# A fused image/text block on one core: mixer centring folded into the projection weights, attention normalisation taken from the inverse deviation before it

## The reference

```python
h = concat(patch_projection(x) + pos_emb, txt)        # 1 + 196 + 77 tokens
# mixer: two selective scans (forward, backward) over the tokens
xn = layernorm(h)                                     # no gain, no offset
r  = xn + mamba_fwd(xn) + mamba_bwd(xn)               # each ends in a projection (out_proj)
h2 = h + (r - mean(r)) * rsqrt(var(r) + eps) * ln_g + ln_b
# transformer block on a normalised input
x  = layernorm(h2)
x  = x + attention(ln(x) * n1_g + n1_b)               # 12 heads of 16 channels
x  = x + mlp(ln(x) * n2_g + n2_b)                     # erf-gelu, 768 hidden
out = h2 + x
```

## Time and profile before

| | |
|---|---|
| median of 3 runs | 6137.19 us (6126.9 to 6150.05) |
| span of the profiled execution | 6123.8 us (13.4 below the median) |
| DVE busy | 5554.8 us, 91% |
| PE busy | 5309.5 us, 87%, granted clock 0.874 of full |
| ACT busy | 3780.6 us, 62% |
| DMA | 16.6% of 16 engines on the main queue |

### The profile page before, as it was taken

One profiled execution on the slowest core, in us unless ns is written; L12 is line 12 of the kernel. 1 busy time (PEld: TensorE's weight loads), 2 busy tenths in 40 slices (PEclk: granted clock), 3 DMA queues, 4 the chain that ended last, 5 costly groups with the idle time before them and its releaser, 6 DMA issues.

```text
span 6123.8 us, 74116 instructions
## 1 busy us (share of the span) xinstructions
PE 5309.5 (87%) x22816; PEld 3509.9 (57%) x22816; DVE 5554.8 (91%) x6069; ACT 3780.6 (62%) x9506; POOL 0.8 (0%) x8
## 2 busy tenths in 40 slices
PE   5788888888888888888889999888998989989888
PEld 3555555555555555555556655655656556556554
DVE  6999999999999999999999999998999989999962
ACT  3566666656666556666666666666666666666643
POOL 0000000000000000000000000000000000000000
PEclk7898888888888888888989988898888888889885
DMA  3211211211211211211221111111111212112100
GB/s 101 64 45 57 64 45 53 66 51 51 64 52 46 66 58 44 65 53 44 65 65 42 60 60 38 64 58 44 64 45 54 66 37 65 50 47 65 40 23 2
DMA packets 56934, 327.85 MB, mean 54 GB/s; under 512 B 13246, under 2 KB 15742, under 8 KB 23627
## 3 DMA queue, kind: packets, MB, share of 16 engines
q1 hardware_dynamic: 56490, 322.53, 16.6%
HBM read 313.52 MB, written 8.98 MB: 53 GB/s over the span
## 4 chain that ended last, share of the span: by engine, by line
PE 40%; DVE 33%; issue 20%; ACT 6%; DVEq 1%; DMA 0%; SPq 0%; ACTq 0%
DVE hs L953 12%; PE y_ps L417 10%; PE f_ps L530 7%; DVE hs L936 4%; PE f_ps L542 4%; DVE hs L957 4%; PE f_ps L581 3%; PE f_ps L496 2%; PE a_ps L455 2%; DVE neg_max L1062 2%; DVE xc L1016 2%; PE f_ps L511 2%; PE f_ps L592 2%; PE f_ps L487 2%; PE a_ps L465 1%
## 5 line engine op out<-in xcount | busy, mean ns | idle before, releaser
L953 DVE TENSOR_TENSOR_SCAN hs<-decay,hs 128x2192 f32<-128x2192 f32 x384 | 1811.1, 4717 | 28.0 <-issue 19.7
L417 PE MATMUL y_ps<-hs,ident 128*128 128x274 f32 x5376 | 1719.8, 455 | 89.5 <-issue 31.3
L715 ACT ACTIVATE decay<-dt,inner_s 128x273 f32<-128x273 f32 x3072 | 1380.6, 513 | 75.7 <-issue 40.3
L417 PEld LDWEIGHTS y_ps<-hs,ident 128*128 128x128 f32 x5376 | 1104.1, 217 | 480.8 <-issue 187.8
L936 DVE TENSOR_TENSOR hs<-b_rows,dtu 128x2192 f32<-128x2192 f32 x384 | 935.5, 2436 | 99.2 <-PE y_ps L417 76.7
L957 DVE TENSOR_TENSOR hs<-hs,c_rows 128x2192 f32<-128x2192 f32 x384 | 934.7, 2434 | 3.4
L530 PE MATMUL f_ps<-qk 16*92 16x274 f32 x2304 | 733.5, 458 | 227.9 <-ACT hid L788 216.4
L805 ACT ACTIVATE hid<-f_ps 92x273 f32<-92x273 f32 (+1 forms) x1152 | 421.7, 393 | 556.6 <-PE f_ps L542 552.4
L788 ACT ACTIVATE hid<-f_ps,neg_max 92x274 f32<-92x274 f32 x1152 | 544.0, 480 | 301.1 <-DVE neg_max L1062 300.9
L530 PEld LDWEIGHTS f_ps<-qk 16*92 16x92 f32 x2304 | 350.7, 174 | 549.2 <-ACT hid L788 344.6
L542 PE MATMUL f_ps<-ident,hid 92*92 92x92 f32 x3456 | 514.7, 286 | 86.8 <-ACT hid L805 48.7
(11 more groups left out here) (103 smaller groups left out, 5773.8 us busy)
## 6 DMA issues: line engine op xcount, KB each, us to landing
b_rows<-bc_rows SPq DMA_DIRECT2D x128, 1096.0 KB, 5.6
c_rows<-bc_rows SPq DMA_DIRECT2D x128, 1096.0 KB, 5.6
xp<-in_patches SPq DMA_DIRECT2D x32, 588.0 KB, 7.4
out<-h SPq DMA_DIRECT2D x32, 205.5 KB, 2.2
bc_rows<-bc_s SPq DMA_DIRECT2D x64, 34.2 KB, 1.5
h<-in_txt SPq DMA_DIRECT2D x32, 57.8 KB, 2.3
w_in_s<-in_w_in SPq DMA_DIRECT2D x1, 1152.0 KB
fc_s<-in_fc SPq DMA_DIRECT2D x2, 576.0 KB
```

The source lines that it names most:

```text
L417: mm = pe.matmul(y_ps[:, 0:T], ident[:, :], hs[q % 2][:, n, :], start=(q % 2 == 0 and n == 0), stop=(q % 2 == 1 and n == end - 1))
L715: e = act.activation(decay[half][:, n, t], dt[d][:, u, t], ACT.Exp, scale=inner_s[:, d, u, s:s + 1])
L953: dve.tensor_tensor_scan(i, a, i, 0.0, ALU.mult, ALU.add).then_inc(scan_done, 1)
```

## The change

1. Once, at the start, DVE subtracts from every row of `w_out` its mean over the 192 output channels (6 sums, 1 scaling, 6 subtractions). The mixer's output, and with it `res`, then has mean zero. LayerNorm 0 no longer needs its centring matmuls: ACT squares `res` straight from SBUF at gap 4, and DVE scales `res` from SBUF.
2. LayerNorm 2 loses its centring matmuls, its squares and its mean-of-squares matmuls. In their place ACT computes `rstd_n` from `rstd_f` with three activations (`second_rstd`), and DVE scales `res` from SBUF.
3. The gap constants move: LayerNorm 0 ends at gap 5 (6 before), LayerNorm 1 at 7 (8), LayerNorm 2 at 8 (10), and everything from QK on is two gaps earlier, so that the fine part ends at gap 38 instead of 40. In the step of b+1 the last two pieces (`add_mlp`, `last_sum`) so stand at gaps 1 and 2 instead of 3 and 4.

```diff
-        CONSTS = 20
+        CONSTS = 29
-        CENTRE_GAPS = (5, 7, 9, 32)
-        VAR_GAPS = (6, 8, 10, 33)
-        QK_GAPS = (11, 17, 22)
+        CENTRE_GAPS = (6, 30)
+        VAR_GAPS = (5, 7, 31)
+        N1_GAP = 8
+        QK_GAPS = (9, 15, 20)
...
-        PROJ_GAP = 30
-        FC1_GAPS = (34, 35)
-        GELU_GAP = 36
-        FC2_GAPS = (37, 38)
+        PROJ_GAP = 28
+        FC1_GAPS = (32, 33)
+        GELU_GAP = 34
+        FC2_GAPS = (35, 36)
+        ADD_GAP = 37
...
+            def second_rstd(f):
+                wait(act, f_y, at(f, 4, -1))
+                act.wait_ge(f_rstd, at(f, 3, 2))
+                act.activation(rstd_n[:, :], rstd_f[:, :], ACT.Square, scale=EPS ** 0.5).then_inc(n1_step, 1)
+                act.wait_ge(n1_step, at(f, 2, 1))
+                act.activation(rstd_n[:, :], rstd_n[:, :], ACT.Ln, scale=-1.0, bias=n1_c[:, 0:1]).then_inc(n1_step, 1)
+                act.wait_ge(n1_step, at(f, 2, 2))
+                act.activation(rstd_n[:, :], rstd_n[:, :], ACT.Exp, scale=-0.5).then_inc(n1_rstd, 1)
...
+                if gap == 4:
+                    squares(res[:, :, :], sq_f, r_ready, at(f, 1, 1), f_sq)
...
-                    scale_by((cen, res, cen, cen)[j], f_ps[0:CH, 0:2, 0:T], rstd_f, f_rstd, at(f, 4, j + 1), f_y)
+                    scale_by((cen, res, cen)[j], (res[:, :, :], f_ps[0:CH, 0:2, 0:T], f_ps[0:CH, 0:2, 0:T])[j],
+                             rstd_f, f_rstd, at(f, 3, j + 1), f_y)
...
+                if gap == N1_GAP:
+                    dve.wait_ge(f_y, at(f, 4, 2))
+                    scale_by(cen, res[:, :, :], rstd_n, n1_rstd, at(f, 1, 1), f_y)
+                    affine(f, 0, small)
...
+                for u in range(UNITS):
+                    dve.tensor_reduce(out_mean[:, u:u + 1], w_out_s[:, u // IC, u % IC, :], AX_X, ALU.add)\
+                        .then_inc(s_c, 1)
...
+                for u in range(UNITS):
+                    a = dve.tensor_scalar(w_out_s[:, u // IC, u % IC, :], w_out_s[:, u // IC, u % IC, :],
+                                          out_mean[:, u:u + 1], None, ALU.subtract)
```

More of the change, by code:

```diff
@@ L155, in build @@
         rstd_f = sb("rstd_f", [CH, T])
+        rstd_n = sb("rstd_n", [CH, T])
+        out_mean = sb("out_mean", [128, UNITS])
+        n1_c = sb("n1_c", [CH, 1])
         xi = sb("xi", [128, IC, XI_W])
@@ L239, in build @@
         f_rstd = sem("f_rstd")
+        n1_step = sem("n1_step")
+        n1_rstd = sem("n1_rstd")
         f_y = sem("f_y")
@@ L280, in build @@
         SP_PARTS = ((0, 2), (2, 3))
-        CENTRE_GAPS = (5, 7, 9, 32)
-        VAR_GAPS = (6, 8, 10, 33)
-        QK_GAPS = (11, 17, 22)
-        V_GAP = 12
-        SCORE_GAPS = [13 + hd + hd // 4 for hd in range(HEADS)]
-        TURN_GAPS = [gap + 2 for gap in SCORE_GAPS]
-        AV_GAPS = (19, 24, 29)
-        PROJ_GAP = 30
-        FC1_GAPS = (34, 35)
-        GELU_GAP = 36
-        FC2_GAPS = (37, 38)
+        CENTRE_GAPS = (6, 30)
+        VAR_GAPS = (5, 7, 31)
+        N1_GAP = 8
+        QK_GAPS = (9, 15, 20)
+        V_GAP = 10
+        SCORE_GAPS = [11 + hd + hd // 4 for hd in range(HEADS)]
+        TURN_GAPS = [gap + 2 for gap in SCORE_GAPS]
+        AV_GAPS = (17, 22, 27)
+        PROJ_GAP = 28
[3 more added lines that the diff above has]
+        ADD_GAP = 37
         VARIANTS = [(CH, 2, (0, 1)), (CH, 1, (2,)), (C // 3, 1, (0,))]
@@ L500, in f_var_mm @@
             def f_var_mm(f, j):
-                pe.wait_ge(f_sq, at(f, 4, j + 1))
+                pe.wait_ge(f_sq, at(f, 3, j + 1))
                 mean_mm(f_ps[:, 2, :], sq_f, f_var)
@@ L597, in fine_early @@
             def fine_early(f, small, gap):
-                if gap == 40 and small:
+                if gap == ADD_GAP + 1 and small:
                     fc2_mms(f, small, 2, (0,))
@@ L604, in fine_early @@
                     j = CENTRE_GAPS.index(gap)
-                    f_centre_mm(*[(res, r_ready, at(f, 1, 1)), (h2, h2_ready, at(f, 1, 1)), (res, f_y, at(f, 4, 2)),
-                                      (res, x3_step, uneven(f, small, 2, 5, 5 if small else 2))][j])
+                    f_centre_mm(*[(h2, h2_ready, at(f, 1, 1)),
+                                  (res, x3_step, uneven(f, small, 2, 5, 5 if small else 2))][j])
                 if gap in VAR_GAPS:
@@ L832, in fine_mid @@
                     j = VAR_GAPS.index(gap)
-                    rstd(f_ps[0:CH, 2, 0:T], rstd_f, f_var, at(f, 4, j + 1), f_ln, at(f, 4, j + 1), f_rstd)
+                    rstd(f_ps[0:CH, 2, 0:T], rstd_f, f_var, at(f, 3, j + 1), f_ln, at(f, 3, j + 1), f_rstd)
+                    if j == 1:
+                        second_rstd(f)
                 if gap == QK_GAPS[0]:
@@ L844, in fine_late @@
                     j = CENTRE_GAPS.index(gap)
-                    squares(f_ps[0:CH, 0:2, 0:T], sq_f, f_cen, at(f, 4, j + 1), f_sq)
+                    squares(f_ps[0:CH, 0:2, 0:T], sq_f, f_cen, at(f, 2, j + 1), f_sq)
+                if gap == 4:
+                    squares(res[:, :, :], sq_f, r_ready, at(f, 1, 1), f_sq)
                 if gap in QK_GAPS[1:]:
@@ L1133, in fine @@
                     j = VAR_GAPS.index(gap)
-                    scale_by((cen, res, cen, cen)[j], f_ps[0:CH, 0:2, 0:T], rstd_f, f_rstd, at(f, 4, j + 1), f_y)
+                    scale_by((cen, res, cen)[j], (res[:, :, :], f_ps[0:CH, 0:2, 0:T], f_ps[0:CH, 0:2, 0:T])[j],
+                             rstd_f, f_rstd, at(f, 3, j + 1), f_y)
                     if j == 0:
                         add_mixer(f)
-                    if j >= 2:
-                        affine(f, j - 2, small)
+                    if j == 2:
+                        affine(f, 1, small)
+                if gap == N1_GAP:
+                    dve.wait_ge(f_y, at(f, 4, 2))
+                    scale_by(cen, res[:, :, :], rstd_n, n1_rstd, at(f, 1, 1), f_y)
+                    affine(f, 0, small)
                 if gap in SCORE_GAPS:
@@ L1144, in fine @@
                     add_attention(f, small)
-                if gap == 39:
+                if gap == ADD_GAP:
                     add_mlp(f, small)
-                if gap == 40:
+                if gap == ADD_GAP + 1:
                     last_sum(f, small)
@@ L1208, in front @@
                                           ALU.mult).then_inc(s_c, 1)
+                for u in range(UNITS):
+                    dve.tensor_reduce(out_mean[:, u:u + 1], w_out_s[:, u // IC, u % IC, :], AX_X, ALU.add)\
+                        .then_inc(s_c, 1)
+                dve.wait_ge(s_c, 26)
+                dve.tensor_scalar(out_mean[:, :], out_mean[:, :], 1.0 / C, None, ALU.mult).then_inc(s_c, 1)
+                dve.memset(n1_c[:, :], 1.0 + EPS).then_inc(s_c, 1)
+                dve.wait_ge(s_c, 28)
+                for u in range(UNITS):
+                    a = dve.tensor_scalar(w_out_s[:, u // IC, u % IC, :], w_out_s[:, u // IC, u % IC, :],
+                                          out_mean[:, u:u + 1], None, ALU.subtract)
+                a.then_inc(s_c, 1)
                 dve.wait_ge(s_c, CONSTS)
```

## The result

The changed kernel is slower: 6214.94 us median (6206.68 to 6222.78) against 6132.05 for the kernel before on the same chip, ratio 1.0127 with a 95% interval of 1.0093 to 1.0161 (the plain quotient of the two medians is 1.0135, inside that interval). The span of the profiled execution is 6204.9 us, 81.1 more than the 6123.8 of before. Lines have moved: 496 is now 503 (centring), 405 is 412 (mean of squares), 487 is 494 (out-projection), 581 is 588 (fc1), 936 is 956, 953 is 973, 957 is 977, 983 is 1003, 715 is 722.

What follows compares the result with a forecast made beforehand. DVE, busy 91%, and its waits were taken as the bound. Large elements -34, small without MLP -29, MLP +91, drain -10, start +4 gave +22 us: span 6146, about 6159 us median, range 6080 to 6215.

Steps and rivals of the forecast that it cites:

- Scalings from SBUF: Two of DVE's four scalings read SBUF instead of PSUM: 718 ns against 716 ns, no gain.
- LayerNorm 3 at gap 31: DVE's wait at the scaling goes, as the mean of squares precedes the out-projection: gain 1.75 us per element.
- State sums at gap 30: DVE's wait for PE's state sums shrinks at gap 30: gain 1.3 us per element, bounds 0.5 and 1.9.
- LayerNorm 0: Gaps 4 to 6: DVE waits 1.3 us; large elements gain 0.3 us, small ones lose 1.3.
- Heads: First heads at gaps 11, 12: 0.5 us waits; last heads leaving gaps 25 to 27: 0.7 back per small element.
- MLP of a small element: Next step's gaps 0 and 1: DVE waits 3.2 us for state sums, 3.7 for exponentials; loss 6.3 without a jump.
- rival C: TensorE's clock falls at fc1 and gap 32's out-projection: some 2 us for each of 30 elements, 6218 us; chance 0.15.
- MLP of a large element: Same count with 12 rows per fc1 group: loss 0.2 us, or 1.2 at TensorE's low clock; 0.7 taken.
- Behind the jump: Where the loop jumps (5 of 14 places), 14 us of DVE waits against 7.0 before: loss 7.0 each.
- Drain and start: Drain gains 10 us from shorter exposed LayerNorm chains; constants at the start lose 4 us ahead of PE's first matmul.
- Rival B: The MLP block finds room and costs nothing at gaps 0 and 1: -69 us, 6068 us; chance 0.20.
- Rival D: Nothing on the path: gains and losses go into other waits of DVE, 6137 us; chance 0.05.

Runs made afterwards that it cites:

- e8: e3 with 16 matmul rows that nobody reads added at gap 4, ahead of LayerNorm 0's mean of squares; 6075.43 us, ratio 0.9911 to the kernel before.
- e2: The changed kernel with only fc1, GELU, fc2 and the last adds put back to gaps 34 to 40; 6119.76 us, ratio 0.9974 to the kernel before.
- e3: The changed kernel with the out-projection of the first four units at gap 31 instead of 32, ahead of fc1; 6106.06 us, ratio 0.9953 to the kernel before.
- e5: The changed kernel with 10 matmul rows that nobody reads added at gap 32, ahead of fc1; 6126.79 us, ratio 0.9991 to the kernel before.
- e1: The changed kernel with all gap constants of the kernel before, so the algebra alone; 6094.4 us, ratio 0.9932 to the kernel before.
- e4: The changed kernel with the GELUs at gap 35 instead of 34, behind the next scan's last two exponentials; 6234.0 us, ratio 1.0159 to the kernel before.

## Why the prediction was right or wrong

The measured time lies inside the range by 0.06 us (6214.94 against 6215), and two of the four executions lie outside it (6222.31 and 6222.78): that is luck. The likeliest case, 6159 us and no change that can be told, was 56 us too low, and "slower" had a chance of 0.35, less than the 0.47 of "no change".

Where the 59 us between the forecast of +22 and the measured +81 on the span stand, by the starts of gap 0: start and first step +2.5 against +2; the large steps 1 to 15 -4.3 against -32; the steps 16 to 30 +93.2 against +62; from gap 0 of the last step on -10.3 against -10. So half of the miss is gain that did not come in the large elements, and half is the small ones. The parts of the forecast:

- *Scalings from SBUF.* Right: DVE's busy time is 5556.3 against 5554.8 us, with 3.3 us of new constants in it, and the two scalings from SBUF take 725 and 719 ns, the two from PSUM 700 and 714. The gain of the Trainium skill's table (VectorE: DVE Perf Modes, the section on the TRN2 errata) does not show.
- *LayerNorm 3 at gap 31.* Right: -1.75 in every element, no idle time at its scaling.
- *State sums at gap 30.* Wrong in size, and the largest single reason for the large elements' half: I gave 1.3 back per element, 40 us in all. The waits there were 1.3 us on average; they are 1.0 in large elements and 0.9 in small ones, so some 0.3 went and 31 us of the forecast gain are missing. My count had PE and DVE arrive within 0.4 us of each other, too close to call it free. No experiment was made on this gap, so why the sums are late there stays open.
- *LayerNorm 0.* Right: 1.0 to 1.6 us at gap 5, forecast 1.3, at the low level of the clock. I named the clock here and did not carry it on: the centring of LayerNorm 1 is late by it too, 0.2 to 0.5 us at gap 7 in 14 steps and 1.4 and 1.8 in two more, most of which e8 took back.
- *Heads.* 0.9 us more at the row maxima of gap 12 in 18 of the 31 steps and nothing in the others, so the forecast 0.5 on average; but in the large steps further small waits come at later heads, 0.9 more per step in all. The softmax wait at gap 27 is gone: forecast 0.7 for small elements only, measured 27.3 to 7.5 us over the kernel.
- *MLP of a small element.* The mechanism was right, place by place: sums at gap 0, exponentials at gap 1. Mis-sized was PE's chain. Its 18.8 us from the affine to the state sums was made of rows at 2.4 GHz; measured it is 23.0 (from 4447.4 to 4470.4, when DVE is released): 4.0 us more for fc1's first group and 0.6 for the out-projection, and 0.4 less for what follows. The wait at gap 0 became 7.4 instead of 3.2 us, the one at gap 1 4.0 instead of 3.7: 11.4 where I had 6.9. By the prediction's own sign (fc1's 18 rows over 6 us) this is rival C, which I held apart as if either the order or the clock decided; they add up. That its 6218 lies 3 us from the measured time is partly luck: I priced it at 2 us for each of 30 elements from 8 rows, but the small elements' group cost 2.3 to 4.2 us more, and in 12 of the 16 large ones the rows ran at the high level.
- *MLP of a large element.* Forecast +0.7 each. Behind a jump `add_mlp` now waits 2.0 to 2.3 us in four places, and 6.8 and 7.0 in the two where fc1's rows ran at the low level, 22.5 together; but the scan's waits behind the jump, six of some 3.3 us (19.7), are gone, which the forecast had not counted.
- *Behind the jump.* I expected 14 us of waits at gaps 0 to 2; measured 6.3 + 4.2 + 1.8 = 12.3, and 7.0 before. The loss there, 5.3, was forecast as 7.0, in spite of the clock.
- *Drain and start.* Drain -14 against -10, start +3.6 against +4.

Rival B (the block finds room, 6068 us) is out by the result: the waits at gaps 0 and 1 are there. Nor would its other terms have come in full: with the MLP back in its old gaps e2 measures 6119.76. Rival D is out by the result too. What is left open: e3 and e5 both change whether PE stands still, and e5 keeps a part of the low level, so how much of e3's gain over e5, 0.4%, is the order itself and how much the clock has not been separated. That e1 beats e3 by 0.2% is inside their intervals.

## What to carry to other kernels

Before matmuls are taken out or moved earlier, look at what TensorE does in front of the next group that something waits for: in this kernel filling a standstill of 2.7 us ahead of fc1 gave 1.3%, more than the algebra saved (e1, 0.7%). Read the granted clock at each such place: the same pause cost nothing in most of the large elements. Price each row at both levels of the clock, and add the slow level to the forecast of the order, not beside it. When a piece moves earlier past others in an in-order queue, count what now stands in front of those others; here the out-projection and two exponentials were that.

## What the runs showed that was not expected

- Ten rows of work that nobody reads (2.47 us on PE per element) made the kernel 1.3% faster, and sixteen more in another place 0.4% (e8 against e3).
- The 8 us at a granted clock of 0.50 came behind a standstill of only 2.71 us; the same standstill was followed by 1.00 in 12 of 16 large elements, and in e3 the clock fell with no standstill at all. In the earlier trace rows the low level followed 7.03 us. In front of LayerNorm 3's centring the standstill is 1.4 us before, and its 8 rows take 2.09 us.
- In e4 a wait of 58.9 us could be taken away entirely and the time did not fall (1.0159 against 1.0127): a wait in front of another, later one says nothing of what its removal gives.
